# Window attention on one core: a split root, statistics from row-order blocks, and a two-bank drain

## What is computed

```
m, s = mean and variance of x over (H, W, 6 channels), for each image and each of 32 groups
xn   = (x - m) / sqrt(s + 1e-5)
q, k, v = windows(xn) @ qkv_w + qkv_b          # 77 tokens to a window, 8 heads
out  = softmax(q @ k.T / sqrt(24)) @ v
x    = x + (out @ proj_w + proj_b)
```

## Time and profile before

| | |
|---|---|
| median of 3 runs | 1455.03 us (1454.76 to 1459.71) |
| time of the profiled execution | 1452.75 us |
| its span, first to last instruction | 1450.9 us |
| mean granted TensorE clock | 0.987 |
| DMA | 109.80 MB, mean 76 GB/s |

### The profile page before, as it was taken

One profiled execution on the slowest core, in us unless ns is written; L12 is line 12 of the kernel. 1 busy time (PEld: TensorE's weight loads), 2 busy tenths in 40 slices (PEclk: granted clock), 3 DMA queues, 4 the chain that ended last, 5 costly groups with the idle time before them and its releaser, 6 DMA issues.

```text
span 1450.9 us, 84355 instructions
## 1 busy us (share of the span) xinstructions
PE 1321.5 (91%) x36480; PEld 1174.7 (81%) x36480; DVE 1049.3 (72%) x2239; ACT 987.0 (68%) x1910; POOL 1027.8 (71%) x1786
## 2 busy tenths in 40 slices
PE   0288899999999999999999999999999999999995
PEld 0277788888888788888888888888888888888884
DVE  5777777777777777777777777777777776666762
ACT  0567677776777677776777767776777667777651
POOL 0547777778777887777777787778777777777433
PEclk9999999999999999999999999999999999999997
DMA  8412233433433334433444334433433322222234
GB/s 146 86 28 57 45 83 83 84 82 71 87 79 81 81 80 86 87 80 64 83 85 83 82 74 85 82 83 75 82 83 62 63 57 59 56 57 59 59 64 107
DMA packets 91236, 109.80 MB, mean 76 GB/s; under 512 B 50018, under 2 KB 83330, under 8 KB 83812
## 3 DMA queue, kind: packets, MB, share of 16 engines
q1 hardware_dynamic: 82996, 72.21, 22.8%
q10 hardware_dynamic: 7872, 32.18, 12.6%
HBM read 71.49 MB, written 31.54 MB: 71 GB/s over the span
## 4 chain that ended last, share of the span: by engine, by line
PE 77%; DVE 10%; POOL 4%; ACT 3%; issue 3%; DMA 2%; SPq 1%; ACTq 0%; POOLq 0%; DVEq 0%
PE ps_a L697 13%; PE ps_b L697 13%; PE ps_q L697 12%; PE ps_k L697 11%; PE ps_a L730 9%; PE ps_s L743 8%; PE ps_s L757 5%; DVE neg_max L633 3%; PE ps_q L793 3%; PE ps_k L826 3%; POOL st_root L331 3%; ACT probs L464 2%; DVE stat L495 2%; DMA x_ring<-in_x 1%; DVE q_hi L659 1%
## 5 line engine op out<-in xcount | busy, mean ns | idle before, releaser
L633 DVE TENSOR_REDUCE neg_max<-ps_s 77x16 bf16<-77x1232 f32 x256 | 369.6, 1444 | 158.1 <-PE ps_s L757 157.7
L373 POOL TENSOR_TENSOR oT_lo<-o,oT_hi 128x308 f16<-128x308 f32 x256 | 193.8, 757 | 266.3 <-ACT oT_hi L458 266.3
L464 ACT ACTIVATE probs<-ps_s,exp_shift,exp_scale 77x1232 f32<-77x1232 f32 x256 | 349.3, 1364 | 5.9 <-PE ps_s L743 4.5
L447 ACT ACTIVATE v_all<-ps_a 77x384 f32<-77x384 f32 x256 | 124.7, 487 | 192.4 <-PE ps_a L697 189.8
L313 POOL TENSOR_TENSOR x_split<-x_norm,x_split 112x128 f16<-112x128 f32 (+1 forms) x496 | 205.8, 436 | 67.1 <-ACT x_split L442 66.8
L697 PE MATMUL ps_a<-wv_hiA,xT 128*128 128x192 f16 x1024 | 213.2, 248 | 6.5 <-ACT num L428 3.4
L340 POOL TENSOR_TENSOR o<-num,inv_all 128x308 f32<-128x308 f32 x256 | 216.2, 845 | 2.9 <-DMA inv_all<-den_dram 2.9
L730 PE MATMUL ps_a<-probs,v_all 77*32 77x77 f32 x8192 | 194.6, 233 | 1.5 <-issue 1.4
L697 PE MATMUL ps_b<-wp_hi,oT_hi 128*112 128x192 f16 x694 | 184.1, 265 | 13.0 <-POOL oT_lo L373 7.5
L697 PE MATMUL ps_k<-xT,wqk_hiA 128*128 128x154 f16 x1024 | 191.4, 235 | 0.0
L648 DVE TENSOR_TENSOR k_lo<-ps_k,k_hi 128x308 f16<-128x308 f32 x256 | 123.1, 481 | 90.1 <-ACT k_hi L453 89.2
(11 more groups left out here) (147 smaller groups left out, 3757.5 us busy)
## 6 DMA issues: line engine op xcount, KB each, us to landing
inv_all<-den_dram SPq DMA_DIRECT2D x1024, 38.5 KB, 2.2
out<-x_ring ACTq DMA_DIRECT2D x248, 115.5 KB
x_ring<-in_x SPq DMA_DIRECT2D x240, 115.5 KB
den<-num SPq DMA_DIRECT2D x256, 4.8 KB
den_dram<-inv SPq DMA_DIRECT2D x256, 4.8 KB
x_ring<-in_x ACTq DMA_DIRECT2D x16, 115.5 KB
out<-x_ring ACTq DMA_DIRECT2D x1, 336.0 KB
out<-x_ring ACTq DMA_DIRECT2D x2, 168.0 KB
```

What stands on the lines that cost most here:

```text
L373: nc.gpsimd.tensor_tensor(oT_tokens(oT_lo, o), by_column(o32[o % 2]), oT_tokens(oT_hi, o), ALU.subtract).then_inc(pool_oT, 1)
L447: nc.scalar.activation(v_all[v % V_BUFS][:, :, 0:HD], ps_a[0:TOK, 0:2 * CH].rearrange("p (h d) -> p h d", d=HD), ACT.Copy)\
L464: nc.scalar.activation(probs[i % 2][:, :, :].rearrange("p g (a n) -> p g a n", a=4), scores(), ACT.Exp, bias=exp_shift[0:TOK, :], scale=ex ...
L633: nc.vector.tensor_reduce(neg_max[:, :, :, HD:HD + 1].rearrange("p a g e -> p g (a e)"), scores(), AXIS.X, ALU.max, negate=True).then_inc( ...
```

## The change

- The power for the root is cut in two instructions of 16 columns each, in slots of lead ROOT 16 and ROOT2 15; NEWTON and RSTD have leads 14 and 13.
- Deviations, squares and second moments take one instruction each (two, one and two before), the square as `scalar_tensor_tensor` with the factor in it and the sum as `tensor_tensor`.
- The first image's statistics come from copies of its four blocks in row order (partition = (r, w), one DMA of 112 partitions per block, on ACT's queue, into ring slots 4 to 7). SP loads the same blocks in column order beside them, with new waits: block 0 after the first two row-order blocks have landed, then `proj_w`, `proj_b`, block 1, then after `stat_read` 1 blocks 4, 5, 2, and after `stat_read` 2 blocks 6, 7, 3.
- The magnitudes of `proj_w` and `proj_b`, the scales that follow from them, `bp_hi`, `bp_lo`, `wp_hi` and `wp_lo` move from ahead of the loop into slots 0 to 8 (DVE 0, 1, 4 and 5, POOL 2 and 8, ACT 6 and 7), and the DMAs of `bp_hi`, `bp_lo` to slot 10.
- The second image's `bn_stats` go in slots 1 to 11, six to a slot.
- Steps 8 to 15 (block 1) are transposed in slots 0, 1, 1, 2, 3, 3, 4, 5 (before: -2 to 5, one to a slot), and their normalising, splitting and copying move with them; odd steps of block 1 use the second bank.
- The last two blocks are projected into two banks (before: the last one), and the last four `oT_lo` are made by DVE.

```diff
-                    at = (h * GROUPS + n) // 5 - 3
+                    at = (h * GROUPS + n) // 6 + 1
...
-M1, DEV, SQ, DEV2, M2, ROOT, NEWTON, RSTD = 20, 19, 18, 18, 17, 16, 15, 14
+M1, DEV, SQ, DEV2, M2, ROOT, ROOT2, NEWTON, RSTD = 20, 19, 18, 18, 17, 16, 15, 14, 13
...
+def x_slot(s):
+    return (0, 1, 1, 2, 3, 3, 4, 5)[s - PAIRS] if PAIRS <= s < 2 * PAIRS else s - X_LEAD
+def steps_at(slot):
+    near = range(slot + X_LEAD - PAIRS, slot + X_LEAD + PAIRS)
+    return [s for s in near if exists(s) and x_slot(s) == slot]
...
+    x_rows = x.rearrange("b (s r) (w c) d -> (b s) (r w) (c d)", r=ROWS, c=WIN_W)
...
         def y_bank(r):
-            return ps_q if r >= N_PAIRS - PAIRS and r % 2 else ps_b
+            return ps_q if r >= N_PAIRS - 2 * PAIRS and r % 2 else ps_b
...
-            for c in range(BLOCKS_IMG):
-                for w in range(NWC // 2, NWC):
-                    load_x(c, w)
-            sp.wait_ge(dma_x[2], landed(2))
-            for c in range(BLOCKS_IMG, 2 * BLOCKS_IMG):
-                for w in range(NWC):
-                    load_x(c, w)
-            sp.wait_ge(dve_bp, 1)
-            sp.wait_ge(pool_wp, 1)
+            sp.wait_ge(dma_stat[0], 2 * 16)
+            load_block(0)
...
+            load_block(1)
+            sp.wait_ge(stat_read, 1)
+            load_block(4)
+            load_block(5)
+            load_block(2)
+            sp.wait_ge(stat_read, 2)
+            load_block(6)
+            load_block(7)
+            load_block(3)
...
-            def root(g):
+            def root(g, half):
                 pool.wait_ge(stat_var, g + 1)
-                nc.gpsimd.tensor_tensor(st_root[:, :], st_var[:, :], half_power[:, :], ALU.pow).then_inc(pool_root, 1)
+                at = slice(half * GROUPS // 2, (half + 1) * GROUPS // 2)
+                nc.gpsimd.tensor_tensor(st_root[:, at], st_var[:, at], half_power[:, at], ALU.pow).then_inc(pool_root, 1)
...
+                    if o == N_PAIRS - LAST + 1:
+                        pool.wait_ge(pool_oT, N_PAIRS - LAST)
+                    reach(pool, dve_oT, o - 1 - (N_PAIRS - LAST))
+                if i < 0:
+                    for x_s in steps_at(i - 1):
+                        copy_one(x_s)
+                if i == 2:
+                    pool.wait_ge(proj_big, 1)
+                    nc.gpsimd.partition_all_reduce(p_big[:, :], p_own[:, :], 128, RMAX).then_inc(proj_big, 1)
+                for n in steps_at(i + 2):
+                    if n >= PAIRS:
+                        normalise(n)
+                if i == PAIRS:
                     pool.wait_ge(act_wp, 1)
                     minus(wp_lo[:, :, :], p32[:, :, :], wp_hi[:, :, :]).then_inc(pool_wp, 1)
...
             for c in range(BLOCKS_IMG):
-                for w in range(NWC // 2):
-                    nc.scalar.dma_start(column(c, w), x_blk[c, w, :, :]).then_inc(dma_x[c % RING], 16)
+                nc.scalar.dma_start(x_ring[:, BLOCKS_IMG + c, :, :].rearrange("p c d -> p (c d)"), x_rows[c, :, :])\
+                    .then_inc(dma_stat[c // 2], 16)
...
             def square(g):
-                link(tt(st_sq[:, :, :, :], st_dev[:, :, :, :], st_dev[:, :, :, :], ALU.mult))
+                link(nc.vector.scalar_tensor_tensor(out=st_sq[:, :, :, :], in0=st_dev[:, :, :, :], scalar=float(N_PART),
+                                                    in1=st_dev[:, :, :, :], op0=ALU.mult, op1=ALU.mult))
             def second_moments(g):
-                for h in range(2):
-                    last = nc.vector.scalar_tensor_tensor(out=st_dev[:, h, :, :], in0=st_sq[:, h, :, :], scalar=float(N_PART),
-                                                          in1=parts(g)[:, h, :, :, 2], op0=ALU.mult, op1=ALU.add)
+                tt(st_dev[:, :, :, :], st_sq[:, :, :, :], parts(g)[:, :, :, :, 2], ALU.add).then_inc(stat_dev, 1)
...
-            dve.wait_ge(dma_w, 4 * 16)
-            dve.wait_ge(dma_rows, 6 * 16)
+            dve.wait_ge(dma_w, 5 * 16)
...
+            def output_weights():
+                dve.wait_ge(dma_rows, 5 * 16)
+                link(nc.vector.tensor_reduce(p_own[:, :], p32[:, :, :].rearrange("p j c -> p (j c)"), AXIS.X, ALU.max,
+                                             apply_absolute_value=True))
+                ts(p_own[:, :], p_own[:, :], 1e-30, None, ALU.max).then_inc(proj_big, 1)
+
+            def output_scale():
+                link(nc.vector.tensor_reduce(bp_big[:, :], bp[:, :], AXIS.X, ALU.max, apply_absolute_value=True))
+                link(nc.vector.reciprocal(scale_inv[:, :], big[:, 2:3]))
+                link(ts(bp_big[:, :], bp_big[:, :], 1.0 / BIAS_ROOM, None, ALU.mult))
+                link(tt(bp_big[:, :], bp_big[:, :], scale_inv[:, :], ALU.mult))
+
+            def output_inverse():
+                dve.wait_ge(proj_big, 2)
+                link(tt(p_big[:, :], p_big[:, :], bp_big[:, :], ALU.max))
+                nc.vector.reciprocal(big_inv[:, 3:4], p_big[:, :]).then_inc(dve_scales, 1)
+                link(tt(out_scale[:, :], big[:, 2:3], p_big[:, :], ALU.mult))
+                link(nc.vector.reciprocal(scale_inv[:, :], out_scale[:, :]))
+
+            def output_bias():
+                link(ts(bp[:, :], bp[:, :], scale_inv[:, :], None, ALU.mult))
+                link(copy(bp_hi[:, :], bp[0:1, :]))
+                tt(bp_lo[:, :], bp[0:1, :], bp_hi[:, :], ALU.subtract).then_inc(dve_bp, 1)
...
+                o = i - O_LAG
+                if N_PAIRS - LAST <= o < N_PAIRS:
+                    dve.wait_ge(act_oT, o + 1)
+                    tt(oT_tokens(oT_lo, o), by_column(o32[o % 2]), oT_tokens(oT_hi, o), ALU.subtract).then_inc(dve_oT, 1)
```

More of the change, by code:

```diff
@@ L70, in exists, with steps_ahead_of @@
     return 0 <= index < limit
+def x_slot(s):
[3 more added lines that the diff above has]
+    return [s for s in near if exists(s) and x_slot(s) == slot]
+def steps_ahead_of(slot):
+    return sum(x_slot(s) < slot for s in range(3 * PAIRS)) if slot < PAIRS else min(slot + X_LEAD, N_PAIRS)
 def stat_groups(slot):
@@ L206, in x_bank @@
         def x_bank(s):
-            return ps_b16 if s < PAIRS and s % 2 else ps_k16
+            return ps_b16 if s < 2 * PAIRS and s % 2 else ps_k16
         def xT_psum(bank, c):
@@ L241, in _, with load_x, load_block @@
             for row in (CB, CB + ROW_G):
-                sp.dma_start(bias_in[row:row + 1, :], b_row).then_inc(dma_rows, 16)
+                sp.dma_start(bias_in[row:row + 1, :], b_row).then_inc(dma_w, 16)
+            def load_x(c, w):
+                sp.dma_start(column(c, w), x_blk[c, w, :, :]).then_inc(dma_x[c % RING], 16)
+            def load_block(c):
+                for w in range(NWC):
+                    load_x(c, w)
+            sp.wait_ge(dma_stat[0], 2 * 16)
+            load_block(0)
             p_rows = proj_w.rearrange("(j g d) c -> g d j c", g=NG, d=HD)
@@ L372, in _ @@
+                if i >= 0:
+                    for x_s in steps_at(i - 1):
+                        copy_one(x_s)
+                if exists(o, N_PAIRS - LAST):
                     pool.wait_ge(act_oT, o + 1)
@@ L376, in _ @@
                 if g is not None:
-                    root(g)
+                    root(g, 0)
+                g = image_at(i, ROOT2)
+                if g is not None:
+                    root(g, 1)
         @block.scalar
@@ L466, in _ @@
                         .then_inc(act_exp, 1)
+                if i == PAIRS - 2:
+                    act.wait_ge(dve_scales, 3)
+                    nc.scalar.activation(p32[:, :, :], p32[:, :, :], ACT.Copy, scale=big_inv[:, 3:4]).then_inc(act_scaled, 1)
+                if i == PAIRS - 1:
+                    act.wait_ge(act_scaled, 2)
+                    nc.scalar.activation(wp_hi[:, :, :], p32[:, :, :], ACT.Copy).then_inc(act_wp, 1)
                 c, r = divmod(i - P_LAG - PAIRS, PAIRS)
@@ L490, in group_stats @@
                 one, two = BLOCKS_IMG * g + 2 * h, BLOCKS_IMG * g + 2 * h + 1
-                if n == 0:
+                if g == 0:
+                    one, two = one + BLOCKS_IMG, two + BLOCKS_IMG
+                    if n == 0:
+                        dve.wait_ge(dma_stat[h], 2 * 16)
+                elif n == 0:
                     dve.wait_ge(dma_x[one % RING], landed(one))
```

136 lines of the change are left out of this document (64 added, 72 removed).

## The result

The median went from 1454.79 us (20 runs, 1452.29 to 1462.16) to 1445.14 us (20 runs, 1435.81 to 1459.68): ratio 0.9936, 95% interval 0.9918 to 0.9953. The forecast was 1417, and its range ended at 1436. So the sign was right, the size a quarter of what was forecast. The profiled execution took 1441.38 us with a span of 1439.6, that is 11.3 less than before.

What follows compares the result with a forecast made beforehand. PE, 91% busy, bounds the middle except where other engines make it wait. Root 20.0 + moments 5.6 + start net of early slots 11.2 + drain 0.8 = 37.6 us, giving 1417; own range 1408 to 1425, 8 in 10 1404 to 1436.

Steps and rivals of the forecast that it cites:

- Root: POOL's power in seven images: two halves of 2.8 us instead of 5.43 end the stalls, gain 20.0 us (13 to 25).
- Newton's two parts move one slot on: Root's slots: Newton's move and DVE's later maximum behind it cost 0.4 us an image (0 to 0.8).
- Slots 0 to 11: First twelve slots: statistics and output scales now on DVE's chain there give back 6.0 us (4 to 10).
- The moments: DVE's statistics in seven images: fewer instructions for deviations, square and second moments gain 5.6 us (2 to 7).
- The rule on the lock: DVE instructions with two SBUF inputs blocked during POOL's SBUF reads: square again 0.85, leaving 0.3 to 0.5 us an image.
- The start: Before the first maximum: row-order loads at 250 GB/s bring statistics earlier, first maximum at 57.5 instead of 74.70, 17.2 us earlier.
- Rival A: Start: row-order loads no faster, bound by what SP's columns also need; start gives -4.3, time 1431; chance 0.18.
- the 168 GB/s: Start: row-order load rate if only the DMA engine count mattered, 147 x 16/14; second half would end near 46.
- The drain: Kernel's end: last low part on DVE takes 0.45 instead of 0.74 and its queue goes, gain 0.8 us (0.3 to 3).
- Rival B: Root: second half late by 2 us, low clock follows again, root's gain -2 instead of 20: 1439; chance 0.08.
- Rival C: Root: power costs per instruction, not per column, so each half takes 5.43 us: 1477, slower; chance 0.05.
- Rival D: Slots 0 to 5 cost 12 instead of 6, with a low clock after one of DVE's stretches: 1424; chance 0.07.

Runs made afterwards that it cites:

- 1: Changed kernel with Newton's first part one slot later (lead 13, both parts in one slot): 1426.40 us, ratio 0.9797 to the kernel before.
- 6: Changed kernel with three waits of POOL on its own last result in the slot of Newton's first part: 1426.60 us, ratio 0.9812 to before.
- experiment 9: Changed kernel with Newton at 13, POOL's two reductions joined ahead of its loop, column loads of blocks 6, 7, 3 spread over slots 0 to 7: 1419.26 us, ratio 0.9750.
- 4: Changed kernel with the power whole again in one instruction and Newton at lead 15 as before: 1443.36 us, ratio 0.9916 to the kernel before.
- 5: Changed kernel with Newton at 13 and POOL's two reductions joined ahead of its first TENSOR_TENSOR: 1425.22 us, ratio 0.9790 to the kernel before.
- experiment 7: Changed kernel with Newton at 13 and the drain's edits (low parts on DVE, second bank of block 30) undone: 1429.86 us, ratio 0.9806 to before.

## Why the prediction was wrong

- **Root, 20.0 forecast, 4.4 in the profile.** The step that failed reads "Newton's two parts move one slot on, from slots that were stretched anyway, and DVE's maximum comes later behind them; I put 0.4 on this (0 to 0.8)". By the slots Newton's place cost 2.2 us an image more than a slot later (8.3 against 6.1), for L585 alone took 3.10 and not the 0.48 to 0.75 of before (experiments 1 and 6). What the forecast said of the halves held: 2.9 against 2.8, no stall in slot one, and in slot two ACT waited 0.38 to 0.72 us for `o`, against 0.45. It weighed POOL's lateness only for those who wait for POOL's results. An engine that is late also runs without pauses, and that held up one that waits for nothing of it. Rows of before had the sign of it: the earlier trace rows has 0.78 for 64 columns, and the text read this as waiting for POOL, then priced Newton's step in a fully packed POOL slot as if it were not there.
- **Slots 0 to 11, 6.0 forecast, 12.2 in the profile.** "ACT's, POOL's and PE's added work of slots 0 to 5 lies in their idle time": the reduction's 0.38 us do, the 5.8 and 7.3 us around it don't. Without them (experiment 9) the term is 5.4.
- **The median above the profile.** The forecast added 2.3 us from the span's execution to the median, for before; after it is 3.8, with a longer tail: up to 14.5 us above the median, where before has 7.4. Slots 0 to 2 now lie beside the column loads, and in some executions PE's program comes late. That is shown in the profiled executions of 4, 5 and 6, with stops of 3.2 to 6.1 us; for the changed kernel's own slow executions it is inferred from their times.
- **The moments, 5.6 against 4.8.** Right within its bounds; the square, taken at 0.3, stayed at 0.86. The rule on the lock, which the text set aside for the 0.35 mean of the earlier trace rows, was right for the square: 0.35 is the mean of 0.45 and 0.23 in turn.
- **The start, 17.2 against 18.8.** Right in its mechanism, earlier statistics through faster row-order loads; the rate was 262 to 297 GB/s instead of 250. That the size is so near is in part luck: statistics that ended 3.6 us before the forecast paid for a chain of moments that took 1.5 longer. Rival A is refuted, and so are the 168 GB/s that the forecast worked out from 16/14: 112 partitions against 14 brought a factor near 1.9.
- **The drain, 0.8 forecast.** No gain is seen; open within some 5 us either way (experiment 7).
- **Rival B** named 2.0 us of lateness and a low clock. The lateness was 0.5 and the low clock came in one image of seven; it had the size of the loss nearly right (-2 for the root against the +4.4 measured) for the wrong reason. Rival C is refuted by 2.9 us a half. Rival D had the size, 12 against the 12.2 measured, and a low clock with it, but its cause was DVE's stretches; it was POOL's reduction that made these slots long.

With the three pieces moved, the sum of 37.6 came to 35.2 in the profile and to 36.6 us of the medians of its own runs (1455.85 to 1419.26). So the gains were there. In the changed kernel they were lost to two waits that no row of before priced: DVE's for POOL in the root, 13 us by the slots, and POOL's around the reduction, some 7.

## What to carry to other kernels

When work makes an engine late, ask not only who waits for its results but whether it still pauses: a DVE instruction with two SBUF inputs can stand for several POOL instructions in a row. Moving it out of the busy stretch, or letting POOL wait for itself for 0.07 us, gave 18 to 20 us here. Keep POOL's cross-partition reductions together, ahead of its first TENSOR_TENSOR. When an engine's first work moves into the time of a burst of loads, take out of the burst what isn't needed yet, for PE's program came over the same DMA engines, and up to 9.9 us late.
